# First group of tokens: b2q and b2k laid beside their weights, x loaded in halves, the first products by parts, output banks marked first, mu's factors spread behind the first scores

## The chip, the cores and the metric

One core of a Trainium2 chip. The metric is the device time of one execution in microseconds. The kernel before took a median of 651.53 us in 3 runs (651.19 to 652.03). The engines are TensorE (PE: matmuls, and PEld: its weight loads), VectorE (DVE), ScalarE (ACT), GpSimd (POOL) and SyncE (SP). DMAs are issued from two queues here: SP's, and ACT's.

## What is computed

Two layers with a residual and a layer norm behind each, for x of 4 sequences of 2048 tokens of 256 values. Cut to what the change touches:

```python
def mlp(x, W1, b1, W2, b2):
    return gelu(x @ W1 + b1, exact) @ W2 + b2
q, k, v = mlp(x, ...q), mlp(x, ...k), mlp(x, ...v)
scores = tril(q @ k.T / sqrt(256 * 512))
x1 = layernorm(x + layernorm(scores @ v) * ln_w + ln_b)
# second layer: soft mixture of experts
xn = layernorm(x1) * gamma + beta
logits = (l2norm(xn) * scale) @ l2norm(mu, axis=0)
# dispatch and combine by softmax over tokens and over slots,
# experts gelu(slot @ w1 + b1) @ w2 + b2
out = layernorm(x1 + combine @ slot_out)
```

## The kernel before

The 8192 tokens are 64 tiles of 128, in 16 groups of 4 tiles (512 tokens). The first part of the kernel does the attention layer group by group; each engine runs its own hand-written order of work (body), group 0 unrolled with attend=False, group 1 unrolled as the "opening" one, and the rest in a loop. Group g computes its hidden layers, keys and values while group g-1 is attended. The second part, the experts, follows after group 15.

Float32 products are made of three fp32r ones: each operand is split into hi and lo, and split3 (L687) issues hi*hi, hi*lo and lo*hi into one bank of PSUM. In group 0 the hi parts of x come from ACT (round_x, L554), the lo parts from DVE (split_first_x, L976), and both parts of each weight from DVE (split_weight, L969): a 128x512 cast (L971) and a 128x512 subtraction (L973).

W2q and W2k are never applied to tokens: fold_weights (L717) makes M = W2k W2q^T, with b2q as two further columns of the moving operand (258 columns, KC), and ku from b2k spread over 128 columns (b2k_wide, spread_b2k L989). Keys are then made by project_k (L739) from the hidden layer and M. fold_weights writes banks 6, 7 (out_ps) and 5 (state_ps); split_m (L995) takes lo parts and copies ku to ku_rows.

What sets the order at the start:

- SP issues xT of group 0 (512 KB), W1k, W1q, W2k, W2q, W1v, W2v, three bias rows, x, and the tensors of the second layer (L426 to L443). ACT issues nine small DMAs first (L540 to L549): three rows of biases, four columns of b2q and two of b2k, each column 128 values of 4 bytes, one to a partition. Only then comes its own work: the table load and a warming activation (L679), round_x(0), and a copy of the turned biases (L623).
- PE: turn_biases (L876) waits for the three rows of biases, transposes them and waits for ACT's copy; then hidden(WK1, 0), hidden(WK1, 1), fold_weights, hidden(WQ1), hidden(WV1), project_k, project_v and turn_k. After the last of these, mark_out (L731) writes both output banks with a float32 product of ident and causal (a start=True write over the whole bank, so that later partial writes accumulate); then the biases of the experts are turned and the squares of mu summed (sum_mu_squares, L898). Between groups 0 and 1 PE waits for mu_floored (L955).
- DVE: split_weight(WK1), split_first_x, split_weight(WQ1), spread_b2k, split_weight(WV1), split_weight(WV2), a wait for the three bias rows, then body(0).
- Group 1 on PE: hidden(WK1) twice, spread_mu_factors (L890, waits for DVE's mu_diag), scores of group 0 (24 matmuls), hidden(WQ1) twice, a wait for mu_united (DVE's mu_units, L1064), chunk 0. The factors come by a chain: PE's sums, DVE's floor_mu (L1045), POOL's power (L532), DVE's mu_factors (L1050).

Hidden layers, keys and values of a group are 14 jobs that take banks 0 to 3 in turn, so a job waits for the readers of the job four before. Jobs 0 to 5 of group 0 are the six hidden products: job 2 (WQ1, half 0) is in bank 2, job 3 (WQ1, half 1) in bank 3.

## Time and profile before

| | |
|---|---|
| median of 3 runs | 651.53 us (651.19 to 652.03) |
| profiled execution: its own time | 651.5 us |
| its span | 649.7 us |
| PE busy | 621.2 us, 96% of the span |
| DVE, ACT, POOL busy | 435.8, 412.7, 343.9 us |
| mean granted clock of TensorE | 0.997 |
| bytes moved by DMA | 30.23 MB, mean 47 GB/s |

The profiled execution lasts 1.8 us longer than its span, which begins with the first instruction and ends with the last landing. Times in rows are microseconds from the span's start. Matmuls are pipelined: the duration of one in the trace includes its way through the array, so the distance between two starts is what one costs in a dense stretch. A row of the timeline can stand for several instructions (xN).

### The profile page before, as it was taken

To read this page: it belongs to the slowest core of one execution; us is meant where nothing else is said; L and a number is where in the kernel's file an instruction comes from. 1 tells how busy PE (TensorE), PEld (TensorE's weight loads), DVE (VectorE), ACT (ScalarE), POOL (GpSimd) and SP (SyncE) were. 2 spreads that over 40 slices of the span, in tenths; PEclk is the share of its full clock that TensorE was granted. 3 is DMA by queue.
4 is the path that set the end of the run, shared out by engine and by line. 5 is a ranking of instruction groups with operands and counts; after the bars stand their busy time and mean duration, and the time that the engine had idled before them with its cause. 6 is when DMAs were issued, how large, how long until landed. Compare 5 with 4: busy or idle time off the path is not lost. (4 is left out here: it accounts for less than half of the span.)

```text
span 649.7 us, 12649 instructions
## 1 busy us (share of the span) xinstructions
PE 621.2 (96%) x4228; PEld 573.6 (88%) x4228; DVE 435.8 (67%) x975; ACT 412.7 (64%) x921; POOL 343.9 (53%) x359
## 2 busy tenths in 40 slices
PE   3999999999999999999999999989999999979994
PEld 2889999999999999999999999989999999968883
DVE  4467676776776777767767767788555556346874
ACT  3645767667667666676676666576766666434675
POOL 2625765675657666656576666475533343103443
PEclk9999999999999999999999999999999999999998
DMA  7311112112111111121111110003000000031444
GB/s 220 98 34 34 33 33 67 33 33 66 32 32 32 32 65 32 32 65 32 32 32 36 61 34 1 2 1 67 1 1 0 0 0 2 1 66 65 146 146 163
DMA packets 30159, 30.23 MB, mean 47 GB/s; under 512 B 6158, under 2 KB 26028, under 8 KB 30124
## 3 DMA queue, kind: packets, MB, share of 16 engines
q1 hardware_dynamic: 29248, 29.78, 15.3%
q8 instruction: 19, 0.31, 0.2%
q10 hardware_dynamic: 876, 0.01, 0.1%
q14 instruction: 16, 0.13, 0.1%
HBM read 21.39 MB, written 8.39 MB: 46 GB/s over the span
## 5 line engine op out<-in xcount | busy, mean ns | idle before, releaser
L565 ACT ACTIVATE h_hi<-bank,bias_col 128x512 fp32r<-128x512 f32 x96 | 66.3, 690 | 36.7 <-PE bank L691 36.6
L487 POOL TENSOR_TENSOR h_lo<-xn_all,h_hi 128x512 fp32r<-128x512 f32 x32 | 41.7, 1302 | 78.3 <-ACT xn_all L567 78.2
L689 PE MATMUL bank<-xnT_hi,w_hi 128*128 128x512 f32 x192 | 77.9, 406 | 4.7 <-DVE xnT_lo L979 4.5
L690 PE MATMUL bank<-xnT_lo,w_hi 128*128 128x512 f32 x192 | 76.6, 399 | 0.0
L691 PE MATMUL bank<-xnT_hi,w_lo 128*128 128x512 f32 x192 | 76.6, 399 | 0.0
L1042 DVE TENSOR_TENSOR state_lo<-bank,state_hi 128x512 fp32r<-128x512 f32 x57 | 39.2, 687 | 47.6 <-ACT state_hi L606 47.6
L1418 PE MATMUL bank<-xn_all,e_tok 128*128 128x257 f32 x256 | 66.4, 382 | 0.2
L1324 ACT ACTIVATE e_tok<-bank,shift,xinv 128x256 f32<-128x256 f32 x64 | 36.1, 565 | 44.9 <-PE bank L1401 24.3
L985 DVE TENSOR_TENSOR h_lo<-bank,h_hi 128x512 fp32r<-128x512 f32 x64 | 44.0, 689 | 30.3 <-ACT bank L567 30.3
L1498 DVE COPY ET_all<-bank 128x256 f32<-128x256 f32 (+1 forms) x64 | 27.0, 424 | 53.2 <-PE bank L1412 52.7
L493 POOL TENSOR_TENSOR ktok_lo<-xn_all,ktok_hi 128x512 fp32r<-128x512 f32 x32 | 38.2, 1194 | 44.7 <-ACT ktok_hi L582 44.7
L606 ACT CAST state_hi<-bank 128x512 fp32r<-128x512 f32 x57 | 33.5, 587 | 41.2 <-PE bank L808 41.2
L1490 PE MATMUL bank<-w_sb,ET_all 128*128 128x256 f32 x256 | 55.5, 379 | 0.8 <-ACT w_sb L1363 0.8
L1490 PEld LDWEIGHTS bank<-w_sb,ET_all 128*128 128x128 f32 x256 | 48.6, 190 | 7.6 <-ACT w_sb L1363 1.1
L499 POOL TENSOR_TENSOR v_lo<-xn_all,v_hi 128x512 fp32r<-128x512 f32 x32 | 41.5, 1298 | 25.4 <-ACT v_hi L597 25.4
L219 POOL TENSOR_TENSOR xn_all<-xn_all,b_rows 128x1024 f32<-128x1024 f32 x16 | 35.0, 2188 | 27.2 <-DVE xn_all L212 27.2
L597 ACT CAST v_hi<-xn_all 128x512 fp32r<-128x512 f32 x32 | 19.9, 622 | 44.5 <-DVE xn_all L1022 44.5
L1399 PE MATMUL bank<-mu_hi,xnT_hi 128*128 128x256 f32 x128 | 47.2, 369 | 0.8 <-POOL blank L1279 0.8
L1418 PEld LDWEIGHTS bank<-xn_all,e_tok 128*128 128x128 f32 x256 | 43.6, 190 | 4.3 <-ACT slot_inT L1346 0.9
L482 POOL TENSOR_TENSOR x_all<-x_all,lnb_rows 128x512 f32 (+1 forms) x32 | 41.1, 1306 | 11.5 <-DMA x_all<-in_L_attn_x 11.5
L689 PEld LDWEIGHTS bank<-xnT_hi,w_hi 128*128 128x128 f32 x192 | 36.5, 190 | 11.0 <-ACT bias_col L623 4.5
L691 PEld LDWEIGHTS bank<-xnT_hi,w_lo 128*128 128x128 f32 x192 | 36.4, 190 | 8.9
(185 smaller groups left out, 2187.7 us busy)
## 6 DMA issues: line engine op xcount, KB each, us to landing
xn_all<-in_xT SPq DMA_DIRECT2D x16, 512.0 KB, 3.7
x_all<-in_L_attn_x SPq DMA_DIRECT2D x16, 512.0 KB, 3.5
out<-xn_all SPq DMA_DIRECT2D x16, 512.0 KB, 2.9
w_sb<-in_L_ffn_w SPq DMA_DIRECT2D x2, 512.0 KB, 5.3
xn_all<-in_L_ffn_w SPq DMA_DIRECT2D x2, 512.0 KB, 6.1
x_all<-in_L_attn_W1k SPq DMA_DIRECT2D x1, 256.0 KB, 4.5
x_all<-in_L_attn_W1q SPq DMA_DIRECT2D x1, 256.0 KB, 5.5
x_all<-in_L_attn_W2k SPq DMA_DIRECT2D x1, 256.0 KB, 5.5
```

Of the source, the lines that this page charges most:

```text
L482: pool.tensor_tensor(xp, xp, lnb_rows[:, :].unsqueeze(1).to_broadcast([P, 2, D]), ALU.add).then_inc(xb_ready, 1)
L487: pool.tensor_tensor(h_lo[:, V_SLOT, m, :], hv[:, m, :], h_hi[:, V_SLOT, m, :].bitcast(F32), ALU.subtract).then_inc(hv_split, 1)
L499: pool.tensor_tensor(v_lo[:, pair, :], v_tok[:, pair, :], v_hi[:, pair, :].bitcast(F32), ALU.subtract).then_inc(v_split, 1)
L565: nc.scalar.activation(h_hi[:, h_slot(j, n), m, :], ps, ACT.Gelu, bias=bias(n, m))
L689: nc.tensor.matmul(ps, w[0], xs[0], start=start, stop=False, skip_group_check=shared)
L690: nc.tensor.matmul(ps, w[0], xs[1], start=False, stop=False, skip_group_check=shared)
L691: return nc.tensor.matmul(ps, w[1], xs[0], start=False, stop=stop, skip_group_check=shared)
L985: nc.vector.tensor_tensor(h_lo[:, h_slot(j, n), m, :], job_bank(j, job)[:, :], h_hi[:, h_slot(j, n), m, :].bitcast(F32), ALU.subtract).the ...
L1042: nc.vector.tensor_tensor(lo[:, :, :], state_halves, hi[:, :, :].bitcast(F32), ALU.subtract).then_inc(state_split, 1)
L1399: nc.tensor.matmul(ps, hi, mu_hi[:, kb, :], start=(kb == 0), stop=False)
L1418: last = nc.tensor.matmul(fold_ps[s][:, 0:D + 1], e_tok[:, t % 4, s * P:(s + 1) * P], xn[q][:, t % GT, :], start=(t == 0), stop=(t == TB - 1))
L1490: last = nc.tensor.matmul(mix_ps[k % 2][t][:, 0:D], ET_all[:, s, toks], so[:, k // GB, s, :], start=(s == 0), stop=(s == SB - 1))
```

## The change

1. The host lays b2q twice beside W2q^T and b2k twice beside W2k^T, so that each is one array of 256 x 258 and one DMA. ACT's six column DMAs are gone, and the tile b2k_col.
2. SP's order is W1k, the two halves of xT (a DMA and a semaphore for each), W2k, W2q, W1q, W1v, W2v, and the rest as before.
3. PE runs mark_out before turn_biases, and behind it first_hidden in place of hidden(WK1, 0) and hidden(WK1, 1): the same 12 matmuls, ordered so that those with hi parts only come first (4), then those with lo parts of the weight (4), then those with lo parts of x (4).
4. fold_weights writes banks 4, 5 (m_ps) and 3 (ku_ps), since banks 6 and 7 are marked by then. Job 3 of group 0 now waits for ku_ready, which DVE raises in copy_ku, placed after split_h(WK1, 1).
5. DVE does spread_b2k ahead of split_weight(WQ1), and waits for the bias rows in bias_v instead of ahead of body(0).
6. ACT's square_mu stands ahead of round_x(1) instead of at the end of group 0. PE no longer waits for mu_floored between the groups, and spread_mu_factors comes after the scores of group 0 instead of ahead of them.

```diff
@@ -268,8 +268,8 @@
     w_in = staged[:, 0:8 * D].rearrange("p (a k n) -> p a k n", a=4, k=KB)
-    w2k_in = staged[:, 8 * D:10 * D].rearrange("p (k n) -> p k n", k=KB)
-    w2q_in = staged[:, 10 * D:10 * D + KB * KC].rearrange("p (k n) -> p k n", k=KB)
+    w2k_in = staged[:, 8 * D:8 * D + KB * KC].rearrange("p (k n) -> p k n", k=KB)
+    w2q_in = staged[:, 11 * D:11 * D + KB * KC].rearrange("p (k n) -> p k n", k=KB)
     quarter = GT * (D + 1)
@@ -279,7 +279,6 @@
     m_lo = asb("m_lo", [P, KB, KC], F32R)
-    b2k_col = asb("b2k_col", [P, KB])
     b2k_wide = asb("b2k_wide", [P, KB, P])
@@ -386,6 +386,7 @@
     scores_ps, state_ps = bank[4], bank[5]
+    m_ps, ku_ps = (scores_ps, state_ps), bank[3]
     state_halves = state_ps[:, :].rearrange("p (k d) -> p k d", k=KB)
@@ -423,14 +424,15 @@
-        load_xT(0)
         def load_weight(n, w):
...
         load_weight(WK1, W1k)
+        for kb in range(KB):
+            sp.dma_start(xT_in[:, kb, :], xT_t[:, kb, 0:GTOK]).then_inc(first_loaded[kb], 16)
+        sp.dma_start(w2k_in[:, :, :], W2kT_b.rearrange("(k p) n -> p k n", p=P)).then_inc(fold_loaded, 16)
+        sp.dma_start(w2q_in[:, :, :], W2qT_b.rearrange("(k p) n -> p k n", p=P)).then_inc(fold_loaded, 16)
         load_weight(WQ1, W1q)
-        sp.dma_start(w2k_in[:, :, :], W2kT.rearrange("(k p) n -> p k n", p=P)).then_inc(fold_loaded, 16)
-        sp.dma_start(w2q_in[:, :, 0:D], W2qT.rearrange("(k p) n -> p k n", p=P)).then_inc(fold_loaded, 16)
         load_weight(WV1, W1v)
@@ -541,21 +543,18 @@
                           b_row.rearrange("(k p) -> k p", p=P)).then_inc(bias_loaded, 16)
-        for kb in range(KB):
-            for col in (D, D + 1):
-                act.dma_start(w2q_in[:, kb, col:col + 1], b2q[kb * P:(kb + 1) * P].rearrange(
-                    "(p o) -> p o", o=1)).then_inc(fold_loaded, 16)
-            act.dma_start(b2k_col[:, kb:kb + 1], b2k[kb * P:(kb + 1) * P].rearrange("(p o) -> p o", o=1)
-                          ).then_inc(fold_loaded, 16)
...
         def round_x(g):
-            act.wait_ge(xT_loaded, 16 * (g + 1))
-            if not (isinstance(g, int) and g == 0):
+            first = isinstance(g, int) and g == 0
+            if not first:
+                act.wait_ge(xT_loaded, 16 * g)
                 act.wait_ge(hidden_done, 6 * g)
             for kb in range(KB):
+                if first:
+                    act.wait_ge(first_loaded[kb], 16)
                 nc.scalar.copy(xT_hi[:, kb, :], xT_in[:, kb, :]).then_inc(x_rounded, 1)
@@ -569,7 +568,7 @@
             for kb in range(KB):
-                nc.scalar.copy(m_hi[:, kb, :], out_ps[kb][:, 0:KC]).then_inc(m_rounded, 1)
+                nc.scalar.copy(m_hi[:, kb, :], m_ps[kb][:, 0:KC]).then_inc(m_rounded, 1)
@@ -657,6 +656,8 @@
             hidden(g, j, WV1, 1)
+            if not attend:
+                square_mu()
             if more:
@@ -672,7 +673,6 @@
             if not attend:
-                square_mu()
                 copy_moe_biases()
@@ -689,6 +689,28 @@
             return nc.tensor.matmul(ps, w[1], xs[0], start=False, stop=stop, skip_group_check=shared)
...
+        def first_hidden():
...
+            ws = [[(w_hi[:, WK1, kb, m * P:(m + 1) * P], w_lo[:, WK1, kb, m * P:(m + 1) * P])
+                   for m in range(2)] for kb in range(KB)]
+            ps = [job_bank(0, HK[m])[:, :] for m in range(2)]
+            pe.wait_ge(w_rounded, 1)
+            for kb in range(KB):
+                pe.wait_ge(x_rounded, kb + 1)
+                for m in range(2):
+                    nc.tensor.matmul(ps[m], ws[kb][m][0], xT_hi[:, kb, :], start=(kb == 0), stop=False)
+            pe.wait_ge(w_split, 1)
+            for kb in range(KB):
+                for m in range(2):
+                    nc.tensor.matmul(ps[m], ws[kb][m][1], xT_hi[:, kb, :], start=False, stop=False)
+            for kb in range(KB):
+                pe.wait_ge(x_split, kb + 1)
+                for m in range(2):
+                    last = nc.tensor.matmul(ps[m], ws[kb][m][0], xT_lo[:, kb, :], start=False,
+                                            stop=(kb == KB - 1))
+                    if kb == KB - 1:
+                        last.then_inc(hidden_done, 1)
@@ -706,6 +728,8 @@
                     pe.wait_ge(v_biased, 2 * g)
+            if first and job == 3:
+                pe.wait_ge(ku_ready, 1)
             if job > 3:
@@ -716,21 +740,20 @@
-            pe.wait_ge(fold_loaded, 16 * 8)
+            pe.wait_ge(fold_loaded, 16 * 2)
             for half in range(KB):
                 for kb in range(KB):
-                    last = nc.tensor.matmul(out_ps[half][:, 0:KC], w2k_in[:, kb, half * P:(half + 1) * P],
+                    last = nc.tensor.matmul(m_ps[half][:, 0:KC], w2k_in[:, kb, half * P:(half + 1) * P],
                                             w2q_in[:, kb, :], start=(kb == 0), stop=(kb == KB - 1))
...
             for kb in range(KB):
-                last = nc.tensor.matmul(state_ps[:, 0:KC], b2k_wide[:, kb, :], w2q_in[:, kb, :],
+                last = nc.tensor.matmul(ku_ps[:, 0:KC], b2k_wide[:, kb, :], w2q_in[:, kb, :],
                                         start=(kb == 0), stop=(kb == KB - 1))
...
-            pe.wait_ge(m_split, KB)
             for ps in out_ps:
@@ -913,14 +936,18 @@
             if not attend:
+                mark_out()
                 turn_biases()
-            hidden(g, j, WK1, 0)
-            hidden(g, j, WK1, 1)
+                first_hidden()
+            else:
+                hidden(g, j, WK1, 0)
+                hidden(g, j, WK1, 1)
+            if opening:
+                pe.wait_ge(moe_ready, 2)
+            if attend:
+                scores(a, p, range(GT))
             if opening:
                 spread_mu_factors()
-                pe.wait_ge(moe_ready, 2)
-            if attend:
-                scores(a, p, range(GT))
             if not attend:
@@ -946,13 +973,12 @@
             if not attend:
-                mark_out()
                 pe.wait_ge(moe_loaded, 16 * 6)
...
         pe.wait_ge(masks_ready, 1)
-        run_groups(body, pe, lambda: pe.wait_ge(mu_floored, 1))
+        run_groups(body, pe, lambda: None)
@@ -987,18 +1013,20 @@
         def spread_b2k():
-            dve.wait_ge(fold_loaded, 16 * 8)
+            dve.wait_ge(fold_loaded, 16 * 2)
             for kb in range(KB):
-                nc.vector.tensor_scalar(b2k_wide[:, kb, :], ones[:, :], b2k_col[:, kb:kb + 1], None,
+                nc.vector.tensor_scalar(b2k_wide[:, kb, :], ones[:, :], w2k_in[:, kb, D:D + 1], None,
                                         ALU.mult).then_inc(b2k_spread, 1)
...
                 dve.wait_ge(m_rounded, kb + 1)
-                nc.vector.tensor_tensor(m_lo[:, kb, :], out_ps[kb][:, 0:KC], m_hi[:, kb, :].bitcast(F32),
+                nc.vector.tensor_tensor(m_lo[:, kb, :], m_ps[kb][:, 0:KC], m_hi[:, kb, :].bitcast(F32),
                                         ALU.subtract).then_inc(m_split, 1)
...
+        def copy_ku():
             dve.wait_ge(ku_done, 1)
-            nc.vector.tensor_copy(ku_rows[:, :], state_ps[:, 0:KC]).then_inc(ku_ready, 1)
+            nc.vector.tensor_copy(ku_rows[:, :], ku_ps[:, 0:KC]).then_inc(ku_ready, 1)
@@ -1018,6 +1046,8 @@
         def bias_v(g, j, m):
+            if isinstance(g, int) and g == 0:
+                dve.wait_ge(rows_loaded, 16 * 3)
             dve.wait_ge(v_done, 2 * g + m + 1)
@@ -1085,6 +1115,8 @@
             split_h(g, j, WK1, 1)
+            if not attend:
+                copy_ku()
             if attend:
@@ -1155,12 +1187,11 @@
         split_first_x()
-        split_weight(WQ1)
         dve.wait_ge(masks_ready, 1)
         spread_b2k()
+        split_weight(WQ1)
         split_weight(WV1)
         split_weight(WV2)
-        dve.wait_ge(rows_loaded, 16 * 3)
         body(0, 0, 0, attend=False)
@@ -1637,10 +1668,12 @@
     laid = {name: inputs[name] for name in _NAMES}
-    for name in ("L0_attn_W2q", "L0_attn_W2k"):
-        laid[name] = _np.asarray(inputs[name]).T
+    for name in ("2q", "2k"):
+        b = _np.asarray(inputs["L0_attn_b" + name])[:, None]
+        laid["L0_attn_W" + name] = _np.concatenate([_np.asarray(inputs["L0_attn_W" + name]).T, b, b], axis=1)
+        del laid["L0_attn_b" + name]
     laid["xT"] = _np.asarray(inputs["L0_attn_x"]).reshape(-1, shape[-1]).T
-    for name in [_NAMES[0], "xT", *_NAMES[1:]]:
+    for name in [_NAMES[0], "xT", *(n for n in _NAMES[1:] if n in laid)]:
         a = _np.ascontiguousarray(laid[name])
```

## Rows read from the trace of the kernel before

**Rows 1.** Stretches: bounds, length, busy PE, PEld, DVE, ACT, POOL, granted clock, DMA.

```profile
43.48:560.00 516.52, 513.82 (x3657) 480.73 (x3657) 360.62 (x787) 345.50 (x787) 297.47 (x297) 1.00 0.10 29
```

**Rows 2.** Timeline of PE: start, duration, line, operation, count, idle before and its releaser.

```profile
6.10 0.24 PE L878 MATMUL bank<-ident,bias_rows 6*128 6x6 f32 x1 [6.10 <-DMA bias_rows<-in_L_attn_b1v]
10.82 0.76 PE L689 MATMUL bank<-xnT_hi,w_hi 128*128 128x512 f32 x1 [4.48 <-DVE xnT_lo L979]
...
13.52 0.52 PE L689 MATMUL bank<-xnT_hi,w_hi 128*128 128x512 f32 x1
...
15.03 1.91 PE L722 MATMUL bank<-x_all 128*128 128x258 f32 x8
...
17.45 0.58 PE L689 MATMUL bank<-xnT_hi,w_hi 128*128 128x512 f32 x1
```

**Rows 3.** Timeline of ACT from the start; ACTq is its issue of DMAs.

```profile
4.46 2.71 ACTq L548 DMA_DIRECT2D b2k_col<-in_L_attn_b2k  x1
7.20 1.28 ACT L679 ACT_TABLE_LOAD   x1 [7.20 <-issue]
...
8.73 1.14 ACT L559 CAST xnT_hi<-xn_all 128x512 fp32r<-128x512 f32 x2
9.77 0.16 ACT L623 COPY bias_col<-bank 128x6 f32<-128x6 f32 x1
```

**Rows 4.** Timeline of DVE up to 22 us.

```profile
5.79 0.43 DVE L971 CAST w_hi<-x_all 128x512 fp32r<-128x512 f32 x1 [4.78 <-DMA x_all<-in_L_attn_W1k]
...
9.38 1.29 DVE L979 TENSOR_TENSOR xnT_lo<-xn_all,xnT_hi 128x512 fp32r<-128x512 f32 x2 [2.44 <-ACT xnT_hi L559]
...
14.23 0.69 DVE L973 TENSOR_TENSOR w_lo<-x_all,w_hi 128x512 fp32r<-128x512 f32 x1
...
21.79 0.42 DVE L1001 COPY ku_rows<-bank 128x258 f32<-128x258 f32 x1
```

**Rows 5.** Timeline of SP's queue: issue of xT and of W2v.

```profile
0.81 0.43 SPq L424 DMA_DIRECT2D xn_all<-in_xT  x1
...
3.93 0.47 SPq L428 DMA_DIRECT2D x_all<-in_L_attn_W2v  x1
```

**Rows 6.** DMA issues: tile, queue, count, size, microseconds from issue to landing.

```profile
xn_all<-in_xT SPq DMA_DIRECT2D x1, 512.0 KB, 4.3
...
x_all<-in_L_attn_W2v SPq DMA_DIRECT2D x1, 256.0 KB, 7.9
```

**Rows 7.** Stretches of 1 us, columns as in Rows 1; last the DMA's GB/s.

```profile
4.00:5.00 1.00, 0.00 (x0) 0.00 (x0) 0.00 (x0) 0.00 (x0) 0.00 (x0) 1.00 1.03 356
...
6.00:7.00 1.00, 0.24 (x1) 0.18 (x1) 0.91 (x2) 0.00 (x0) 0.00 (x0) 1.00 0.55 138
```

**Rows 8.** Timeline of POOL: the second mask.

```profile
2.29 0.64 POOL L467 TENSOR_SCALAR_AFFINE_SELECT causal<-causal 128x512 f32<-128x512 f32 x1
```

**Rows 9.** Timeline of PE at the end of group 0 and in group 1.

```profile
29.96 1.88 PE L735 MATMUL bank<-causal,ident 128*128 128x512 f32 x4
...
33.39 0.50 PE L689 MATMUL bank<-xnT_hi,w_hi 128*128 128x512 f32 x1 [0.25 <-DVE mu_n L1047]
...
36.96 0.71 PE L894 MATMUL bank<-mu_diag,ones 128*128 128x128 f32 x4 [0.50 <-DVE mu_diag L1061]
...
40.14 0.44 PE L689 MATMUL bank<-xnT_hi,w_hi 128*128 128x512 f32 x1
...
43.48 0.38 PE L689 MATMUL bank<-v_hi,masked_hi 128*128 128x256 f32 x1 [0.31 <-DVE mu_unit L1066]
```

**Rows 10.** Timeline of DVE in group 1.

```profile
40.34 1.13 DVE L1030 SCALAR_TENSOR_TENSOR bank<-bank,xn_all,causal 128x128 f32<-128x128 f32 x4 [2.84 <-PE bank L691]
...
42.74 0.68 DVE L1066 TENSOR_TENSOR mu_unit<-mu_in,bank 128x512 f32<-128x512 f32 x1
```

**Rows 11.** Timeline of ACT and of POOL at work that the change moves past.

```profile
26.79 0.20 ACT L579 CAST gam_hi<-xn_all 128x4 fp32r<-128x4 f32 x1 [1.05 <-DVE xn_all L1007]
...
31.41 0.63 ACT L616 ACTIVATE mu_unit<-mu_in 128x512 f32<-128x512 f32 x1
```

More of the change, by code:

```diff
@@ L26, with build @@
 BANK = 512
-def build(nc, x, xT, W1q, b1q, W2qT, b2q, W1k, b1k, W2kT, b2k, W1v, b1v, W2v, b2v, ln_w, ln_b,
+def build(nc, x, xT, W1q, b1q, W2qT_b, W1k, b1k, W2kT_b, W1v, b1v, W2v, b2v, ln_w, ln_b,
           gamma, beta, mu, scale, w1, b1, w2, b2, out):
@@ L334, in build @@
             xT_loaded = asem("xT_loaded")
+            first_loaded = [asem(f"first_loaded{kb}") for kb in range(KB)]
             weight_loaded = [asem(f"weight_loaded{n}") for n in range(4)]
@@ L915, in body @@
                     if not attend:
+                        mark_out()
                         turn_biases()
-                    hidden(g, j, WK1, 0)
-                    hidden(g, j, WK1, 1)
+                        first_hidden()
+                    else:
+                        hidden(g, j, WK1, 0)
+                        hidden(g, j, WK1, 1)
                     if opening:
-                        spread_mu_factors()
                         pe.wait_ge(moe_ready, 2)
@@ L923, in body @@
                         scores(a, p, range(GT))
+                    if opening:
+                        spread_mu_factors()
                     if not attend:
```

## The prediction, made before the changed kernel was seen

> **What bounds the kernel now.** I read the stretches first. Between 43.48 and 560 us TensorE is busy 513.82 of 516.52 us at a granted clock of 1.00 [rows 1]: a dense column of matmuls, which the change leaves as it is. So the change is worth what it does to the moment at which PE enters that stretch (chunk 0 of group 0, at 43.48), and any microsecond won there should reach the end. Then I read PE's timeline from zero and asked of each gap what ended it. The reader is to see four things. PE does nothing of weight before 10.82 us; the wait before it ends with DVE's lo part of x [rows 2], which waited for ACT's hi part [rows 4], which ACT began only at 8.73, since its last DMA issue ran from 4.46 to 7.17 and the table load came behind it [rows 3]. The data weren't late: xT was issued at 0.81 [rows 5] and landed 4.3 us later, at 5.1 [rows 6]; W1k was there at 5.79 [rows 4]. Second, the first six matmuls start 0.43 us apart ((13.52 - 10.82)/6 = 0.45 with the first), the six behind them 0.25 ((15.03 - 13.52)/6) [rows 2]: 512 columns in about 0.43 us are the 1.2 GHz level, in 0.23 us the 2.4 GHz one. PE had been all but idle before and ran 2.70 us before it rose, though the granted clock reads 1.00 in these stretches as well [rows 7]. Third, mark_out takes about 1.8 us of PE at the end of group 0. Fourth, in group 1 PE waits 0.25 us for mu_floored, 0.50 for mu_diag and 0.31 for mu_unit [rows 9].
>
> **Start of the first products.** *ACT.* Without six of nine issues its table load can begin near 2.0 us, when the third row of biases has been issued (the six cost 7.17 - 1.98 or so; the load is 1.28, the warming and the step to round_x 0.25 [rows 3]), so it is ready at 3.6 and waits for x. *Landings.* W1k and the halves of xT are the same 768 KB as before in another order. All of it had landed by 5.79 before [rows 4]; W1k now first, I put at 4.4, the first half of xT at 5.1 and the second at 5.8. ACT rounds them in 0.57 each (1.14 for two [rows 3]) up to 6.4. *PE.* mark_out may begin when the masks are made, 2.29 + 0.64 = 2.93 [rows 8]. Its four records cost 1.8 us at the high level [rows 9]; begun by an idle PE I count double, 3.5, thus up to 6.4. The biases landed at 6.10 [rows 2], so this hides it. Then come the transposition (0.24 [rows 2]), ACT's copy (0.16 [rows 3]) and two handoffs of 0.1: the first product starts at 7.05. That x comes in halves and that hi parts go first therefore earns nothing by itself: the bias copy opens last, and the third of the parts, x_lo, is there at 7.1 (6.4 + 0.65 [rows 4]), before PE asks for it at its ninth matmul. Bounds: 6.65 if mark_out is faster, 7.5 if the second half lands at 6.3.
>
> **The first twelve.** At the high level 12 x 0.235 = 2.8 us, so fold_weights begins at 9.85 against 15.03 [rows 2]. I take the high level, as PE will have worked 3.5 us by then against 2.70 when it rose before. At the low level throughout they take 5.1 and end at 12.2; that is the other bound. The fold weights are the third and fourth 256 KB now; they should be there by 8.3, when 1.3 MB have passed at 200 to 350 GB/s, and even the 8.8 of the old order would be early enough.
>
> **Job 3, the new wait.** By PE alone: fold and ku take 17.45 - 15.03 = 2.42 us, job 2 takes 6 x 0.235 = 1.40 (all at the high level [rows 2]), so job 3 could start at 13.7. But it now waits for copy_ku on DVE, and that stands behind split_weight(WV2) and two split_h. W2v was issued at 3.93 [rows 5] and landed 7.9 later, at 11.8 [rows 6]. Now it is issued one DMA later, 0.5, but without 768 four-byte rows of ACT in the same 16 engines. What these cost no row shows alone; from the row at its worst, 138 GB/s between 6 and 7 us against 356 between 4 and 5 [rows 7], the bounds are a landing at 9.6 (2.1 MB in all, 0.85 of them by 5 us, the rest at 0.345 MB per us, and 0.95 for the receipt) and at 12.35. I take 11.0, nearer the middle, since the dip need not be theirs. Then DVE needs 1.15 for the weight (0.43 + 0.69 and a handoff), 0.69 twice for the h_lo, 0.42 for ku and 0.1 [rows 4]: 3.1 us, job 3 starts at 14.1. Before it started at 17.45 + 1.40 = 18.85. **First term: 4.75 us.** Behind the waiting job PE holds WV1 and project_k; ACT's gelus and DVE's m_lo only follow PE there, so all shift with it. ACT's gelus don't bind (job 1 rounded at 12.4).
>
> The Trainium skill, page "DMA: Bandwidth & Descriptors", section "Issuing engines are not separate DMA queues", speaks against the change: issuing on several engines saves only the sequencer's time, usually small beside the transfer. By that alone the removed issues bring nearly nothing; the trace shows 5.2 us of that time on ACT with xT already landed, so it doesn't hold here. The same page, "Specifications", says that under 512 B a DMA does read-modify-write; if the dip is theirs, W2v lands at 9.6, PE decides, the first term is 5.15 and the sum 643.7.
>
> **Moved at no cost.** square_mu, 0.63, lands in ACT's idle 1.05 before gam_hi [rows 11]; without that cover it would push k_tok's rounding, and PE would feel at most 0.6. The wait for the bias rows was ahead of nothing that PE needed. xT of group 1 is issued near 13 us, behind x and the second layer's loads in SP's queue; I put its landing at 18, need at 19.9. split_hv on POOL waits for x plus ln_b as before.
>
> **Group 1.** In the old clock, less the first term: mark_out's 1.8 and the 0.25 go, so hidden(WK1) ends at 36.46 - 2.05 = 34.4. The scores (40.14 - 36.96 less the spread's 0.5 = 2.7 [rows 9]) end at 37.1. The factors' chain doesn't start earlier, as POOL ends its v_lo where it did; mu_diag is ready at 36.9, just in time for the spread behind the scores. But DVE is in it until then, so its h_lo (0.69) ends at 37.6 and the masks begin there. From mask to mu_united DVE took 42.74 + 0.68 - 40.34 = 3.1 [rows 10], so 40.7; PE itself, with 0.5 of spread and 2.8 of WQ1, would be at chunk 0 at 40.5. Chunk 0 starts at 40.8, against 43.48. **Second term: 2.65** (of it 1.8 mark_out, 0.25 floor, 0.6 of the two waits). Bounds: 2.05 if the spread waits anew, 2.95 if nothing waits.
>
> **Sum.** 4.75 + 2.65 = 7.4 us. The profiled execution took 651.5 us for a span of 649.7, and the median is 651.53, so: 651.5 - 7.4 = **644.1 us**.
>
> **Rivals.**
> (B) *VectorE's queue decides.* W2v lands at 12.35 or later, job 3 starts at 15.4, and the first term is 3.4: 645.4. For it: one DMA more ahead of it. Against: the six column loads are gone.
> (C) *The level stays low.* PE idles between mark_out and the first product and the twelve run 0.43 apart to 12.2; job 3 at 16.0, first term 2.85: 646.0; half of them, and PE ties with DVE. For it: half a microsecond of light work just before. The Trainium skill ("TensorE: Matmul & The Clock Gate", Part 1) makes the low level the default of an idle array, which sustained work lifts; by it mark_out pays the slow part where nobody waits.
> (D) *More:* no wait for ku and none in group 1, first term 5.4, second 2.95: 643.2.
> (E) *Given back:* a transfer of group 1 (xT, landing at 21 behind the second layer's loads) eats most of the start's gain; about 3 us come back: 647.
> (F) *Slower than before.* fold_loaded: the rows are now 1032 B rather than 1024. If each were cut or rewritten, the two arrays and all behind them in SP's queue crawl. Job 3 waits for W2v through DVE; it decides from a landing at about 18.4 us (18.85 + 2.65 - 3.1), and at 20 us the kernel takes 653.1. Against it: packets of 1 and 2 KB ran at 356 GB/s [rows 7]. That the change doesn't do what it says would be the same place with nothing won: ACT's start bound by something else than its issues, or the issues' time worth as little as the page cited above has it: 651.5, and no row points to it.
>
> **Chances.** Forecast 0.58, B 0.16, C 0.10, D 0.08, E 0.04, F 0.02, no change 0.02. The range takes in D, B and C: 642.9 to 646.4. Below 0.2% (1.3 us, about what a measurement of this kernel can tell) is no change: faster 0.96, same 0.015, slower 0.025.
>
> **What would show it.** ACT's table load near 2 us; the first 128x512 product at 7.0 and the twelve 0.23 apart; fold at 9.9; job 3 at 14.1 with a wait ended by ku's copy on DVE; no mark_out behind project_v; scores, then spread with next to no wait; chunk 0 near 36.0 us; the stretch behind it as long as before. It is wrong if PE's first product waits for something other than the biases, if W2v lands outside 9.6 to 12.4, or if the dense stretch lengthens.

## The result, and the profile after

The changed kernel takes a median of 642.4 us in 4 runs (641.93 to 643.18); the kernel before took 651.36 beside it. The ratio is 0.9863 (95% interval 0.9851 to 0.9874): 9.0 us faster, and 0.5 us below the lower end of the forecast range (642.9). The profiled execution is the fastest of the four, 641.93 us with a span of 640.2, so in the profiles the difference is 9.5 us of span.

The start, in the timelines of PE, ACT and DVE of the changed kernel (start, duration, line, operation, idle before and its releaser):

```profile
2.98 3.48 PE L758 MATMUL bank<-causal,ident 128*128 128x512 f32 x4 [2.98 <-POOL causal L469]
6.39 0.22 PE L901 MATMUL bank<-ident,bias_rows 6*128 6x6 f32 x1
7.00 1.20 PE L702 MATMUL bank<-xnT_hi,w_hi 128*128 128x512 f32 x4 [0.38 <-ACT bias_col L622]
...
9.91 1.91 PE L746 MATMUL bank<-x_all 128*128 128x258 f32 x8
...
13.92 0.40 PE L689 MATMUL bank<-xnT_hi,w_hi 128*128 128x512 f32 x1
```

```profile
1.98 1.28 ACT L679 ACT_TABLE_LOAD   x1 [1.98 <-issue]
...
4.37 0.62 ACT L558 CAST xnT_hi<-xn_all 128x512 fp32r<-128x512 f32 x1 [0.89 <-DMA xn_all<-in_xT]
6.26 0.62 ACT L558 CAST xnT_hi<-xn_all 128x512 fp32r<-128x512 f32 x1 [1.27 <-DMA xn_all<-in_xT]
6.79 0.16 ACT L622 COPY bias_col<-bank 128x6 f32<-128x6 f32 x1
```

```profile
6.91 0.69 DVE L1005 TENSOR_TENSOR xnT_lo<-xn_all,xnT_hi 128x512 fp32r<-128x512 f32 x1 [1.20 <-ACT xnT_hi L558]
...
8.42 0.43 DVE L997 CAST w_hi<-x_all 128x512 fp32r<-128x512 f32 x1 [0.18 <-DMA x_all<-in_L_attn_W1q]
...
10.56 0.42 DVE L997 CAST w_hi<-x_all 128x512 fp32r<-128x512 f32 x1
...
12.97 0.42 DVE L1029 COPY ku_rows<-bank 128x258 f32<-128x258 f32 x1
```

The reader is to see, against [rows 2 to 4]: ACT's table load at 1.98 instead of 7.20; mark_out in time that PE had idle, and mostly at the low level (3.48 us against 1.88 in [rows 9]; its first three products take 0.85 us or more from start to start, the last 0.69); the first product at 7.00 instead of 10.82, behind ACT's bias copy; fold_weights at 9.91 instead of 15.03, since the twelve products run 0.24 us apart from the first on; and job 3 at 13.92 with no wait ahead of it, as DVE's copy of ku was done at 13.39. The second half of xT landed only at 6.24, later than forecast, and DVE's lo part of it ended at 7.60. W2v landed at 9.82, but DVE turned to it only at 10.56: from 8.42, when W1q was there, to 13.39 it worked without a gap.

Group 1 and the first chunk, PE and DVE of the changed kernel, against [rows 9, 10]:

```profile
29.00 0.22 PE L689 MATMUL bank<-h_hi,k_hi 128*128 128x128 f32 x1
...
31.52 0.27 PE L691 MATMUL bank<-h_hi,k_lo 128*128 128x128 f32 x1
31.77 0.71 PE L917 MATMUL bank<-mu_diag,ones 128*128 128x128 f32 x4
...
34.89 0.40 PE L691 MATMUL bank<-xnT_hi,w_lo 128*128 128x512 f32 x1
35.34 0.39 PE L689 MATMUL bank<-v_hi,masked_hi 128*128 128x256 f32 x1
```

```profile
30.26 1.45 DVE L1091 TENSOR_SCALAR mu_diag<-ident,mu_fac 128x128 f32<-128x128 f32 x2
31.63 0.68 DVE L1011 TENSOR_TENSOR h_lo<-bank,h_hi 128x512 fp32r<-128x512 f32 x1
32.23 1.12 DVE L1060 SCALAR_TENSOR_TENSOR bank<-bank,xn_all,causal 128x128 f32<-128x128 f32 x4
...
34.61 0.68 DVE L1096 TENSOR_TENSOR mu_unit<-mu_in,bank 128x512 f32<-128x512 f32 x1
```

None of PE's rows has an idle time, but two short waits hide in the way of the product before through the array. mu_diag ended at 31.71 and PE took it at 31.77, 0.25 us behind the start of the last score, where the scores before it are 0.11 apart. mu_unit ended at 35.29 and chunk 0 began at 35.34, 0.45 behind a product that costs 0.23 in a dense stretch. So PE still waited for DVE, 0.14 and 0.2 us. Chunk 0 began 8.14 us earlier than at 43.48 [rows 9]. The difference of the spans is 9.5, so 1.4 us more were won behind it. The next rows are stretches (bounds, length, busy PE, PEld, DVE, ACT, POOL, granted clock, DMA share, GB/s): first the kernel before, then the changed one, each from the first scores of group 1 to those of group 14, and behind it to the end.

```profile
63.62:400.23 336.61, 336.61 (x2401) 314.37 (x2399) 241.54 (x505) 226.81 (x433) 214.54 (x221) 1.00 0.13 39
400.23:649.70 249.47, 232.56 (x1512) 213.89 (x1510) 157.70 (x397) 154.76 (x428) 101.32 (x102) 0.99 0.14 43
```

```profile
55.39:390.59 335.20, 335.20 (x2401) 313.33 (x2400) 240.86 (x505) 226.44 (x433) 214.32 (x221) 1.00 0.13 40
390.59:640.20 249.61, 232.43 (x1512) 213.73 (x1510) 157.69 (x397) 154.59 (x428) 101.25 (x102) 0.99 0.14 43
```

The same 2401 records of PE, without a gap and at the same granted clock, take 1.41 us less; the rest of the kernel takes 0.1 more. So the account of the profiles is 8.1 up to chunk 0, 0.1 from there to the first scores of group 1, 1.4 in the dense stretch, less 0.1 at the end: 9.5. The forecast had 7.4 for the first and nothing for the third. From here on "the stretch" is this one.

### The profile page after: what moved, and what is told of

The parts are those of the page before. It is cut to its first block and busy times, and to the rows that moved or that the text cites. A ratio compares the mean times of both kernels' runs of the same rounds, so it can differ in the third digit from the quotient of the medians.

```text
span 640.2 us, 12645 instructions
## 1 busy us (share of the span) xinstructions
PE 619.6 (97%) x4228; PEld 571.8 (89%) x4228; DVE 435.4 (68%) x975; ACT 412.1 (64%) x921; POOL 343.4 (54%) x359
## 5 line engine op out<-in xcount | busy, mean ns | idle before, releaser
L689 PE MATMUL bank<-xnT_hi,w_hi 128*128 128x512 f32 x188 | 75.5, 402 | 0.0
L690 PE MATMUL bank<-xnT_lo,w_hi 128*128 128x512 f32 x188 | 74.2, 395 | 0.0
L691 PE MATMUL bank<-xnT_hi,w_lo 128*128 128x512 f32 x188 | 74.2, 395 | 0.0
L566 ACT ACTIVATE bank<-bank,bias_col 128x512 f32<-128x512 f32 x64 | 42.1, 658 | 0.0
```

The lines of the kernel that those rows point to most:

```text
L566: nc.scalar.activation(exact, ps, ACT.Gelu, bias=bias(n, m)).then_inc(h_rounded, 1)
L689: nc.tensor.matmul(ps, w[0], xs[0], start=start, stop=False, skip_group_check=shared)
L690: nc.tensor.matmul(ps, w[0], xs[1], start=False, stop=False, skip_group_check=shared)
L691: return nc.tensor.matmul(ps, w[1], xs[0], start=False, stop=stop, skip_group_check=shared)
```

## The experiments

Each kernel is one edit of the changed kernel, or of the kernel before where that is said. Medians are of the kernel itself; the changed kernel's is 642.4. The edits are shown shortened, with comments added. Part 1, the halves of xT with the order of first_hidden, and the places of mark_out and of the spread were tried by themselves; SP's new order, the new banks of fold_weights and the places of spread_b2k and square_mu were not.

**cols_only**: the kernel before with part 1 alone, the unused tile b2k_col kept.

```diff
-                    act.dma_start(w2q_in[:, kb, col:col + 1], b2q[...])   # x4, and b2k_col x2
+                sp.dma_start(w2k_in[:, :, :], W2kT_b...); sp.dma_start(w2q_in[:, :, :], W2qT_b...)
```

> The kernel before with one part alone: b2q and b2k laid beside their weights, so ACT issues three DMAs instead of nine (the unused tile b2k_col stays, so that all tiles lie where they did). Theory A (ACT's issues held the start): table load near 2.0 us, x rounded from 5.1 us, DVE's lo part of x behind the weight's at 8.25, first product at 8.35 instead of 10.82, still begun at the low clock level; 2.5 us won, 649.0. Rival (issues on ACT cost only small sequencer time, the transfers decide): first product near 10.8, 651.4. On the dense stretch from the scores of group 1 to those of group 14 (336.6 us before, 335.2 after the change): theory L (the place of the tiles in SBUF moved it) expects 336.6 here; theory V (executions differ by as much) expects anything between 335 and 337.

Measured 649.47 us (ratio to before 0.9974, 0.9964 to 0.9983). PE's timeline:

```profile
8.23 0.77 PE L682 MATMUL bank<-xnT_hi,w_hi 128*128 128x512 f32 x1 [2.31 <-DVE xnT_lo L972]
...
12.21 0.54 PE L682 MATMUL bank<-xnT_hi,w_hi 128*128 128x512 f32 x1
...
13.05 1.91 PE L715 MATMUL bank<-x_all 128*128 128x258 f32 x8
```

Theory A holds: 10.82 became 8.23. But nine products ran at the low level here (8.23 to 12.21, 0.44 apart) instead of six, so fold_weights came only 2.0 us earlier, not 2.6. The stretch took 336.60 us, as before.

This kernel also shows what the small rows did to the loads, with SP's order as it was. Its issue of W2v (KB, us from issue to landing) and its stretch from 6 to 7 us:

```profile
x_all<-in_L_attn_W2v SPq DMA_DIRECT2D x1, 256.0 KB, 5.6
```

```profile
6.00:7.00 1.00, 0.00 (x0) 0.00 (x0) 0.96 (x3) 0.26 (x2) 0.00 (x0) 1.00 1.07 360
```

Against [rows 6, 7], the landing takes 5.6 us instead of 7.9, and 360 GB/s pass instead of 138.

**mark_back**: mark_out at the end of group 0 again.

```diff
-                        mark_out()
                         turn_biases()
...
                     if not attend:
+                        mark_out()
                         pe.wait_ge(moe_loaded, 16 * 6)
```

> The changed kernel with mark_out moved back to the end of group 0. Theory A: two prices, 1.8 us for mark_out on PE's path and 1.2 us because the first six products then start 0.43 us apart instead of 0.23: 642.4 + 3.0 = 645.4. Rival: only mark_out's own 1.8 us: 644.2. The first product should still start at 7.0 (ACT's bias copy). Dense stretch: theory L 335.2, theory V anything between 335 and 337.

Measured 645.58 us (0.9911, 0.9895 to 0.9928), 3.2 more than the changed kernel: the rival with 1.8 is out. PE's timeline:

```profile
4.52 0.24 PE L901 MATMUL bank<-ident,bias_rows 6*128 6x6 f32 x1 [4.52 <-DMA bias_rows<-in_L_attn_b1v]
6.61 2.07 PE L702 MATMUL bank<-xnT_hi,w_hi 128*128 128x512 f32 x4 [1.85 <-ACT bias_col L622]
```

The sum expected was 3.0, and its parts came out otherwise. The first product started at 6.61, not at 7.0. All twelve, not six, ran 0.44 apart in the profiled execution, so fold_weights began at 11.90, and chunk 0 came 3.5 us later (38.86). The rows show something about the start as well: the biases were there at 4.52, and PE still waited to 6.61, since ACT copies the biases only behind its rounding of x's second half, which landed at 5.85 and was rounded at 6.50. So mark_out ahead of the first product costs 0.4 us there, and pays for it with the level.

**spread_back**: the factors' spread ahead of the scores.

```diff
                     if opening:
+                        spread_mu_factors()
                         pe.wait_ge(moe_ready, 2)
                     if attend:
                         scores(a, p, range(GT))
-                    if opening:
-                        spread_mu_factors()
```

> The changed kernel with spread_mu_factors ahead of the scores again. Theory A (the factors' chain over POOL does not move with PE, so the wait grows to all that was won before it): PE waits from 28.95 to 31.7 for mu_diag, chunk 0 starts near 38.1 instead of 35.3: 2.7 us lost, 645.1. Rival (the order is worth the 0.5 us that the wait before cost): 642.9. Dense stretch: theory L 335.2, theory V anything between 335 and 337.

Measured 649.66 us (0.9976, 0.9966 to 0.9986), with runs from 647.25 to 650.18: a loss of 7.3 us where 2.7 were expected. PE's timeline and two stretches of the profiled execution (one of the lesser losses, 647.25):

```profile
31.57 0.71 PE L917 MATMUL bank<-mu_diag,ones 128*128 128x128 f32 x4 [2.52 <-DVE mu_diag L1090]
...
33.49 0.41 PE L689 MATMUL bank<-h_hi,k_hi 128*128 128x128 f32 x1
33.70 0.41 PE L690 MATMUL bank<-h_lo,k_hi 128*128 128x128 f32 x1
...
37.01 0.63 PE L691 MATMUL bank<-xnT_hi,w_lo 128*128 128x512 f32 x1
37.43 0.63 PE L689 MATMUL bank<-xnT_hi,w_hi 128*128 128x512 f32 x1
```

```profile
33.30:36.00 2.70, 2.70 (x15) 2.70 (x15) 0.00 (x0) 0.00 (x0) 0.00 (x0) 0.50 0.40 140
36.00:40.00 4.00, 4.00 (x12) 3.13 (x12) 3.58 (x9) 1.64 (x3) 0.00 (x0) 0.50 0.00 0
```

The wait is the forecast one. What came on top is the clock: PE had been idle for 2.52 us, and from 33.3 to 40 us the granted clock is 0.50, the 1.2 GHz level; scores cost 0.21 instead of 0.11 us each and the 128x512 products 0.43 instead of 0.23. It was no accident of one execution: the mean granted clock of the nine runs is 0.988 to 0.992, that of the changed kernel's four 0.995 to 0.997.

**spread_busy**: the same, with PE kept at work in the wait.

```diff
                     if opening:
+                        pe.wait_ge(mu_floored, 1)
+                        for _ in range(5):
+                            nc.tensor.matmul(state_ps[:, D:2 * D], ident[:, :], causal[:, 0:2, :].rearrange(
+                                "p c n -> p (c n)"), start=True, stop=True)
                         spread_mu_factors()
```

> spread_back (scores behind the factors' spread) with five float32 products of 256 columns, about 2.2 us of PE work that nobody reads, into an unused half of the state's bank while PE waits for mu_diag. If the idle stretch of 2.5 us is what lets the clock fall (0.50 granted from 33.3 to 40 us in spread_back), the level stays high, chunk 0 starts near 38.1 and the time is 642.4 + 2.7 = 645.1; if the fall has another cause, it stays near 649.7.

Measured 645.39 us (0.9901, 0.9885 to 0.9917), with a mean granted clock of 0.993 to 0.997 in its four runs, and 1.00 in the profile where it was 0.50 in spread_back (the five products are ten records):

```profile
29.87 2.32 PE L948 MATMUL bank<-causal,ident 128*128 128x256 f32 x10
```

```profile
33.30:36.00 2.70, 2.70 (x26) 2.70 (x25) 0.00 (x0) 0.00 (x0) 0.00 (x0) 1.00 0.56 194
```

Useless work in the same wait wins back 4.3 us. So the idle stretch was the cause of the fall, and the order of the spread is worth 3.0 us for the wait and up to 4.3 more for the clock.

**whole_x**: xT of group 0 as one DMA, the twelve products in the old order.

```diff
-                for kb in range(KB):
-                    sp.dma_start(xT_in[:, kb, :], xT_t[:, kb, 0:GTOK]).then_inc(first_loaded[kb], 16)
+                sp.dma_start(xT_in[:, :, :], xT_t[:, :, 0:GTOK]).then_inc(first_loaded[0], 16)
...
-                        first_hidden()
+                    hidden(g, j, WK1, 0)
+                    hidden(g, j, WK1, 1)
```

> The changed kernel with xT of group 0 as one DMA and the first twelve products in the old order. The prediction's step (halves and parts earn nothing, the bias copy opens last): first product at 7.0 to 7.7, 642.4 to 643.1. Rival, from the trace after the change (the second half landed at 6.26, ACT then needs 1.14 us for two halves and DVE 0.69 for the last lo part): rounded from 6.26 to 7.4, lo part at 8.2, first product at 8.3, 1.3 us lost, 643.7. Dense stretch: theory L 335.2, theory V anything between 335 and 337.

Measured 643.71 us (0.9878, 0.9858 to 0.9897); the four runs are 642.53, 642.87, 644.54 and 645.06. The profiled one is the last:

```profile
2.99 3.78 PE L757 MATMUL bank<-causal,ident 128*128 128x512 f32 x4 [2.99 <-POOL causal L468]
...
7.81 0.77 PE L688 MATMUL bank<-xnT_hi,w_hi 128*128 128x512 f32 x1 [0.84 <-DVE xnT_lo L1002]
...
12.21 0.55 PE L689 MATMUL bank<-xnT_lo,w_hi 128*128 128x512 f32 x1
```

The first product waits for x's last lo part, 0.8 us later than in the changed kernel: the rival's mechanism, with a start between the two that were expected (up to 7.7, or 8.3). The halves by themselves earned nothing in these two profiles. x as one DMA landed at 5.64 and was rounded at 6.86; the two halves landed at 4.29 and 6.24 and were rounded at 6.88. So what earned the time is the order by parts, which asks for the lo parts last. In this execution the level stayed low for ten of the twelve products, up to about 12.2 us, although mark_out had run for 3.8 us. With runs up to 2.5 us apart the median says no more than "about 1" of the price.

**The place of the tiles.** Without b2k_col, 8 bytes that take 32, all tiles behind it (h, k, v, ktok, masked, state among them) lie 32 bytes nearer. Two kernels put the old place under the new kernel, and the new place under the old one:

```diff
 # old_layout: the changed kernel
+            b2k_col = asb("b2k_col", [P, KB])      # unused
             b2k_wide = asb("b2k_wide", [P, KB, P])
 # cols_packed: cols_only
-            b2k_col = asb("b2k_col", [P, KB])      # unused there
```

> The changed kernel with the tile b2k_col (8 bytes, unused) allocated where it was, so that all tiles behind it (h, k, v, ktok, masked, state and others) lie 32 bytes further on, as before the change. Theory L (their place costs 1.4 us in the dense stretch): stretch 336.6 instead of 335.2, 642.4 + 1.5 = 643.9. Rival (something else of the change shortens the loop, such as the phase between the engines): 335.2 and 642.4.

> cols_only without the unused tile b2k_col: the kernel before with its tiles behind b2k_col 32 bytes nearer and with three DMA issues on ACT instead of nine, nothing else. Theory L: dense stretch 335.2 instead of 336.6, 649.5 - 1.5 = 648.0. Rival: 336.6 and 649.5.

Measured 643.68 us (0.9877, 0.9861 to 0.9893) and 648.21 (0.9949, 0.9936 to 0.9962), thus 1.28 more and 1.26 less than the kernels they were made from; stretches 336.62 and 335.18. The stretch follows the tile, whichever of the two kernels it stands in. That of old_layout:

```profile
56.31:392.93 336.62, 336.62 (x2401) 314.37 (x2399) 241.44 (x505) 226.77 (x433) 214.36 (x221) 1.00 0.13 39
```

Three further kernels asked which place and which tiles: pad64 (64 unused bytes ahead of b2k_wide), h_only (32 behind h_lo, so that k and all behind it lie as before), xt_odd (32 ahead of x's hi and lo tiles and 32 behind them).

```diff
 # pad64
+            spare = asb("spare", [P, 16])
             b2k_wide = asb("b2k_wide", [P, KB, P])
 # h_only
+            spare = asb("spare", [P, 8])
             k_hi = asb("k_hi", [P, KB, GTOK], F32R)
 # xt_odd
+        sb("spare_a", [P, 8])
         xnT_hi = [sb("xnT_hi0", [P, KB, GTOK], F32R)]
         xnT_lo = [sb("xnT_lo0", [P, KB, GTOK], F32R)]
+        sb("spare_b", [P, 8])
```

> The changed kernel with 64 unused bytes ahead of b2k_wide: all tiles behind lie 64 bytes further on than in the changed kernel, so their place within 64 bytes is that of the changed kernel (32), while old_layout, 32 bytes on, had 0. If the place within 64 bytes decides, the dense stretch is 335.2 and the time 642.4; if it is the absolute place or any shift away from the changed kernel's, 336.6 and 643.9.

> The changed kernel with 32 unused bytes behind h_lo: h_hi and h_lo stay where the change put them, k, v, ktok, masked and state lie as in the kernel before. If the hidden layers' tiles carry the gain, the dense stretch stays at 335.2 (642.4); if the others do, 336.6 (643.9); if both, in between.

> The changed kernel with 32 unused bytes ahead of xnT_hi0 and 32 behind xnT_lo0: x's hi and lo parts, the moving operands of the 128x512 products, now lie at 32 within 64 bytes as h does, all else keeps its place within 64 bytes. If a moving operand or a written tile is cheaper there in general, the dense stretch is shorter again, by up to 1.4 us (334, 641); if the gain is particular to the tiles behind b2k_col, 335.2 and 642.4; if x was better at 0, longer.

Measured 643.65, 641.52 and 641.74 us, with stretches in this order:

```profile
55.31:391.74 336.43, 336.43 (x2400) 314.47 (x2399) 241.38 (x505) 226.48 (x433) 214.38 (x221) 1.00 0.13 39
```

```profile
56.29:390.89 334.60, 334.60 (x2400) 312.76 (x2399) 241.50 (x505) 226.84 (x433) 214.29 (x221) 1.00 0.12 40
```

```profile
55.98:390.52 334.54, 334.54 (x2401) 312.94 (x2399) 240.86 (x505) 226.30 (x433) 214.15 (x221) 1.00 0.13 40
```

pad64 refutes the idea that the place within 64 bytes decides: it has that of the changed kernel and the stretch of the old one, nearly. h_only was expected at 335.2, at 336.6 or between and came out below both. So the place matters, by up to 2.6 us in 335 (from 334.05, further below, to 336.62), by a rule that these runs don't give.

**The small rows.** cols_back puts six column DMAs of 4-byte rows on ACT's queue ahead of its table load again, cols_late puts them behind it. Both use a new tile that moves the others back to the old place.

```diff
+                for kb in range(KB):
+                    for col in range(3):
+                        act.dma_start(spare_cols[:, 3 * kb + col:3 * kb + col + 1],
+                                      b1q[kb * P:(kb + 1) * P].rearrange("(p o) -> p o", o=1)).then_inc(spare_loaded, 16)
```

> The changed kernel with six column DMAs (128 values of 4 bytes each) on ACT's queue again, into an unused tile, ahead of ACT's table load. Theory A (ACT's issues held the start and the small rows slow the others down): the last issue ends near 7.2 us, x rounded from 8.7, bias copy near 10, first product at 10.1 to 10.3, W2v lands near 11.8: 3.2 us lost, 645.6. If the change's other parts alone carried it: 642.4. The new tile also shifts those behind it by 32 bytes, which by theory L adds 1.5: 647.1.

> The same six DMAs behind ACT's table load and warming. It separates the two costs: table load at 2.0, then six issues. If the small rows in the DMA engines cause the stall of the issues and the dip in bandwidth, the last issue takes over 2 us again, W2v lands at 11.5 or later (10.5 in the changed kernel), and copy_ku on DVE makes job 3 wait; if the transfers are limited by their own bytes, W2v lands near 10.5 and each issue takes 0.45, x rounded from 6.3: first product at 7.7, 643.1; theory L adds 1.5 for the layout.

Measured 647.20 us (0.994, 0.9923 to 0.9958) and 645.92 (0.9926, 0.9906 to 0.9946), stretches 336.60 in both; so 3.5 and 2.2 more than old_layout, which has the same places. Of cols_back, a row of ACT, one of PE, and a stretch:

```profile
6.63 1.28 ACT L686 ACT_TABLE_LOAD   x1 [6.63 <-issue]
```

```profile
9.41 1.72 PE L710 MATMUL bank<-xnT_hi,w_hi 128*128 128x512 f32 x4 [2.59 <-ACT bias_col L629]
```

```profile
10.00:13.00 3.00, 3.00 (x8) 2.31 (x7) 1.98 (x6) 0.00 (x0) 0.00 (x0) 0.50 0.99 225
```

The first product came at 9.41 behind a table load at 6.63. That 647.1 was expected is luck in part: the start came 0.7 to 0.9 us earlier than expected, and the level took back what that won. PE had stood idle for 2.59 us behind mark_out, began the twelve at the high level (0.34 us from the first to the second), and then had a granted clock of 0.50, with at least seven of the twelve 0.43 apart. It is the second trace with a fall behind some 2.5 us without work.

In cols_late ACT has its table early, but the six issues end only at 6.36, and x is rounded from 6.46. Its row of the DMA issues for W2v and its stretch from 6 to 7 us stand first, and then the same of the changed kernel:

```profile
x_all<-in_L_attn_W2v SPq DMA_DIRECT2D x1, 256.0 KB, 8.2
```

```profile
6.00:7.00 1.00, 0.96 (x2) 0.18 (x1) 0.00 (x0) 0.54 (x2) 0.00 (x0) 1.00 0.61 181
```

```profile
x_all<-in_L_attn_W2v SPq DMA_DIRECT2D x1, 256.0 KB, 5.5
```

```profile
6.00:7.00 1.00, 0.62 (x3) 0.14 (x2) 0.09 (x1) 0.68 (x2) 0.00 (x0) 1.00 1.09 339
```

Issued at 4.28 in both, W2v lands at 12.5 with the small rows and at 9.8 without. Some 3 KB in 768 pieces nearly halve the bandwidth for 2 us (181 and then 213 GB/s against 339 and 369), and the issues of both queues stall beside them (2.06 us for W2v on SP, 2.96 for the last three on ACT). But the late landing cost PE nothing, against what was expected: DVE's copy of ku was done at 15.70 and job 3 started at 16.24 without a wait. What cols_late loses up to job 3 is the first product at 7.71 and eight of the twelve at the low level.

**A version that beats both.** bias_late moves PE's wait for the bias copy behind the first twelve products; combined adds h_only's 32 bytes, and combined_xt xt_odd's as well.

```diff
                 def turn_biases():
...
-                    pe.wait_ge(bias_ready, 1)
                 def fold_weights():
+                    pe.wait_ge(bias_ready, 1)
                     pe.wait_ge(fold_loaded, 16 * 2)
```

> The changed kernel with PE's wait for ACT's bias copy moved from ahead of the first products to ahead of fold_weights. By the prediction's step (the bias copy opens last) the first product then starts right behind the biases' transposition, near 6.6 instead of 7.0, but the products of the second half wait for its rounding at 6.9: 0.3 us won, 642.1. Rival: DVE's or ACT's parts open last anyway, 642.4.

> bias_late and h_only together: the changed kernel with PE's wait for the bias copy ahead of fold_weights, and 32 unused bytes behind h_lo. If both effects are real and add up: dense stretch 334.6, first product at 6.9 or earlier, 642.4 - 0.6 - 0.1 to 0.3: 641.6 (641.2 to 641.9). If placement only shifts the loss between tiles by chance of the execution, 642.3.

> combined with xT_odd's 32 bytes ahead of xnT_hi0 and 32 behind xnT_lo0. If the gains of the two placements are independent: dense stretch 334.0 (335.2 less 0.6 less 0.6), 641.0; if each is one step towards the same floor, 334.5 and 641.6; if only absolute places count, anything between 334 and 336.6.

Measured 642.26 us (0.9865, 0.9849 to 0.9882), 641.20 (0.9835, 0.9821 to 0.9849) and 641.13 (0.9837, 0.9823 to 0.9851). bias_late alone can't be told from the changed kernel: its first product started at 6.90, behind the transposition, but one of the twelve and part of the next ran at the low level. And there is little more to win there. In combined_xt, where the first product started at 6.58 and all twelve ran at the high level, job 3 still began at 14.00:

```profile
14.00 0.47 PE L692 MATMUL bank<-xnT_hi,w_hi 128*128 128x512 f32 x1 [0.37 <-DVE ku_rows L1032]
```

That is the wait for DVE's copy of ku that the prediction counted on: it ended last here, with fold_weights 0.4 us earlier than in the changed kernel and W1q landed 0.6 us later (9.02). The stretches are 335.22, 334.60 and

```profile
55.45:389.50 334.05, 334.05 (x2401) 312.98 (x2400) 241.53 (x505) 226.54 (x433) 214.52 (x221) 1.00 0.13 40
```

so the two placements add up in the stretch (334.0 expected), while the times of the last two kernels lie within their scatter of each other. combined, at 0.9835 of the kernel before, is 1.2 us below the changed kernel, and the intervals of the two ratios don't meet (0.9821 to 0.9849, and 0.9851 to 0.9874).

## Why the prediction was right and wrong

**The step that failed is the one that the sum starts from:** that the change leaves the dense stretch as it is. The prediction counted nothing for it, as the work in it is unchanged; it took 1.41 us less, through the 32 bytes of a tile that the change deletes. With the old place the changed kernel takes 643.68, inside the range and 0.4 from the forecast of 644.1. The rows of before don't show it, but the diff line that removes b2k_col stood there, and the prediction gave it no sentence. None of the rivals was this, and the range's lower end had no room for it. The two terms of the sum were 0.74 us too small together; that alone would have stayed inside the range.

**The first product: the right time, in part by luck.** ACT's issues held PE: undone alone they give 2.6 us of start (cols_only), put back they cost 2.4 (cols_back). The first product was forecast at 7.05 and came at 7.00, fold_weights at 9.85 and came at 9.91. But two premises were off. The biases, put at 6.10 as before, were there at 4.52 (mark_back). And x's second half landed at 6.24, not at 5.8, so ACT's copy of the biases came behind that half's rounding, which ended at 6.88. mark_out and the transposition had ended by 6.61. That halves and parts earn nothing was half wrong: DVE's last lo part ended at 7.60, so the old order would have waited 0.6 to 0.8 for it; the parts hide that, the halves do nothing.

**The first term was 5.12, not 4.75.** The mis-sized part of it is the wait of job 3 for ku, which the sum lets end at 14.1 and which never came: PE decided, job 3 moved by as much as fold_weights did (15.03 to 9.91, 19.04 to 13.92), and the 5.15 that the prediction names for this case was right. The start of job 3 before, 18.85 in the sum, was 19.04, as the first product behind ku costs 0.42 and not 0.235; it does so in both kernels and drops out of the 5.15. Two things were off in the wait. W2v landed at 9.82, near the lower bound of 9.6 and not at 11.0; the cause of the dip, left open, was the small rows (cols_only, cols_late). The 0.95 us "for the receipt" in that bound is a size that no row shows; the runs measure the landing as a whole. And it was no longer W2v's landing that DVE waited for, but its own queue since W1q: 0.7 us later, so that the copy of ku was only 0.5 us ahead of job 3.

The sentence of the Trainium skill ("DMA: Bandwidth & Descriptors", "Specifications") on read-modify-write under 512 B points the right way; that 4-byte rows slow their neighbours is shown, and whether they do it by being read and rewritten or by their mere number is not. Its other rule ("Issuing engines are not separate DMA queues") calls the time that issues take on an engine's sequencer usually small; here the six took 5.2 us of ACT and held the first product by 2.6.

**The second term was 3.0, not 2.65.** The mechanism held to the order of events: DVE's chain (mu_diag, h_lo, masks, to mu_united) ended last, as forecast, with 0.2 us of PE waiting. From mu_diag's end it took 3.6 us instead of the 3.8 summed, as operations in a row overlap by some 0.08 us in the trace. Had the spread stayed ahead of the scores, the loss would have been 7.3: the sum priced that move as a wait of 0.5 us and never asked what mark_out's removal would make of it.

**Rival C** (the level stays low) is real, and belongs to single executions: the changed kernel's profile has none of the twelve at the low level, old_layout's three, whole_x's ten. Of the thirteen profiles with mark_out ahead, ten have none to three and three have seven to ten; of the four without it (before, mark_back, cols_only, cols_packed), all have six to twelve. So mark_out ahead helps and promises nothing. A product at the low level costs 0.2 us more, and six of them would make the 1.3 us between the runs of the changed kernel; that this is their cause is not shown, as only one of those runs has a profile. Of D, which has no wait for ku and none in group 1, the first happened and the second all but 0.3 us; its 5.4 for the first term was too much. B, E and F didn't happen: W2v and xT of group 1 were early enough, and nothing crawled.

**What stays open:** why the place of a tile changes what a matmul costs by about 0.6 ns (1.41 us over 2401 records). By the distances between the starts of PE's records, 0.58 of the 1.41 us lie in the hidden products, 0.41 in project_v, 0.23 in project_k and 0.2 in all the rest, and project_k's own three kinds of product move both ways (m_hi with h_hi 0.36 less, m_hi with h_lo 0.23 more). cols_only and old_layout repeat the figures of before, and cols_packed those of the changed kernel, each kind within 0.02 us. So it is not one wait. PE has no idle time in either stretch, and the busy times of DVE, ACT and POOL differ by 0.3% or less. Which tiles meet where in the memory was not tried one by one.

## What to carry to other kernels

Count the issues on every engine that has compute behind them, and the pieces of a few bytes in them, before looking at bytes: six DMAs of 512 bytes, in pieces of 4, held this kernel's start by 2.6 us and took more than half of the bandwidth from 6 to 7 us. A wait that a change leaves on the matrix engine must be priced anew when work ahead of it is removed, with the clock in the price: 2.5 us of idle time cost 3.0 us by themselves and 4.3 by the clock. And a change that adds or deletes even a tiny tile moves all tiles behind it; run one variant with the old layout before explaining a per cent or less.

## What the runs showed of the hardware

The effect of placement repeats exactly: kernels of the old place took 336.60 to 336.62 us for the stretch (5 kernels, the one before among them), those of the new place 335.18 to 335.24 (7 kernels), and other places 336.43, 334.60 (twice), 334.54 and 334.05. The matrix engine's level rises at a different moment in each execution. With the same work from 2.98 on it rose before 6.4 us in the changed kernel and in pad64, and after 8.6 in old_layout and h_only; in whole_x, where PE stood idle for 0.84 us in between, after 12.2. The profile of one execution doesn't tell that. And a fall after 2.5 us without work (spread_back, cols_back) stands in the profile as a granted clock of 0.50, while the low level at the very start stands beside a granted clock of 1.00: there only the distance of the products shows it.
